# Tile statistics taken by the finishing stage, and the order of Wq and the context at the start of two wide attentions

## What is computed

```python
def _layernorm(x, axis=-1, eps=1e-05):
    m = jnp.mean(x, axis=axis, keepdims=True)
    v = jnp.var(x, axis=axis, keepdims=True)
    return (x - m) / jnp.sqrt(v + eps)

x = x + _L0_attn_ref(_layernorm(x), ...)            # windowed self attention
x = x + _L0_xattn_ref(_layernorm(x), ctx_768, ...)  # 16 heads of 64
x = x + _L0_ffn_ref(_layernorm(x), ...)             # mixture, 2 of 8 choices
...                                                 # layers 1, 2 and 3 likewise
```

```python
q = x @ Wq; k = context @ Wk; v = context @ Wv
sim = jnp.einsum('bhid,bhjd->bhij', q, k) * SCALE
attn = jax.nn.softmax(sim, axis=-1)
return jnp.einsum('bhij,bhjd->bhid', attn, v) ... @ Wo + bo
```

## Time and profile before

| | |
|---|---|
| time, median of 3 runs | 2756.67 us (2753.91 to 2758.6) |
| the profiled execution | 2766.99 us, its span 2765.3 us |
| mean granted TensorE clock in it | 0.884 of full speed |
| PE busy | 2137.1 us (77%) |
| DVE busy | 1714.5 us (62%) |
| ACT busy | 1201.0 us (43%) |
| POOL busy | 617.3 us (22%) |

### The profile page before, as it was taken

The page is one execution under the profiler, slowest core; times in us unless marked ns, Lnnn a source line. Parts: engine busy times, 40 slices in busy tenths (PEclk is TensorE's granted clock), DMA queues, the critical chain, the costliest instruction groups (busy, mean ns, idle before and its releaser), DMA issues. The chain is left out here.

```text
span 2765.3 us, 28267 instructions
## 1 busy us (share of the span) xinstructions
PE 2137.1 (77%) x10151; PEld 1327.1 (48%) x10181; DVE 1714.5 (62%) x2529; ACT 1201.0 (43%) x1900; POOL 617.3 (22%) x349
## 2 busy tenths in 40 slices
PE   5688889595699979889473888888758979373894
PEld 3456556584223335668331444444535654252474
DVE  5554345424677745522464999999634776856665
ACT  2334322110276653311145899999713236302340
POOL 3321112120332101012114666564100210000100
PEclk8899799697899999879796999999869999696896
DMA  6553120243654300224200000000111000000001
GB/s 128 77 85 39 59 92 1 102 154 122 105 78 66 34 21 0 73 74 171 68 34 27 1 1 1 1 1 1 61 58 35 0 1 0 0 8 13 8 1 37
DMA packets 107529, 126.74 MB, mean 46 GB/s; under 512 B 14823, under 2 KB 98676, under 8 KB 106357
## 3 DMA queue, kind: packets, MB, share of 16 engines
q1 hardware_dynamic: 94404, 109.63, 17.7%
q10 hardware_dynamic: 10098, 7.71, 0.9%
q0 software_dynamic: 2880, 7.48, 0.7%
...
## 5 line engine op out<-in xcount | busy, mean ns | idle before, releaser
L3148 DVE TENSOR_TENSOR_SCAN l2s_h<-l2s_aw 128x2048 f32<-128x2048 f32 x64 | 290.0, 4532 | 5.2 <-ACT l2s_rs L3193 5.2
L3107 PE MATMUL l2s_big<-g_xn,g_ident 128*128 128x512 f32 x512 | 259.0, 608 | 11.5 <-ACT g_xn L3186 6.4
L3162 POOL TENSOR_SCALAR l2s_aw<-l2s_aw 128x2048 f32<-128x2048 f32 x64 | 211.0, 3298 | 10.3 <-DVE l2s_aw L3140 5.1
L582 DVE TENSOR_REDUCE l1at_nm<-l1at_s 128x1 f32<-128x512 f32 x256 | 162.2, 683 | 66.7 <-PE l1at_s L432 65.7
L3099 PE MATMUL l2s_c_ps<-g_ident,l2s_h 128*128 128x128 f32 x1024 | 148.9, 279 | 55.7 <-ACT g_xn L3186 37.0
L3099 PEld LDWEIGHTS l2s_c_ps<-g_ident,l2s_h 128*128 128x128 f32 x1024 | 117.3, 141 | 146.4 <-issue 86.7
L680 ACT ACTIVATE g_xn<-l1at_s 128x512 f32<-128x512 f32 x256 | 143.4, 598 | 82.2 <-PE l1at_s L456 81.7
L3186 ACT ACTIVATE g_xn<-l2s_c_ps,l2s_ct 128x512 f32<-128x512 f32 x256 | 163.0, 690 | 17.1 <-PE l2s_c_ps L3099 16.9
L582 DVE TENSOR_REDUCE l0at_nm<-l0at_s 128x2 f32<-128x384 f32 x128 | 70.0, 557 | 101.0 <-PE l0at_s L432 99.9
L3179 ACT ACTIVATE l2s_aw<-l2s_dt,l2s_A 128x2048 f32<-128x2048 f32 x64 | 128.3, 2006 | 0.0
L3107 PEld LDWEIGHTS l2s_big<-g_xn,g_ident 128*128 128x128 f32 x512 | 82.0, 190 | 81.8 <-ACT g_xn L3186 58.6
...
## 6 DMA issues: line engine op xcount, KB each, us to landing
l1f_w<-in_L_ffn_w_dram SPq DMA_DIRECT2D x16, 1024.0 KB
l0f_w<-L_ffn_experts_inter_dram SPq DMA_DIRECT2D x7, 1024.0 KB
l0f_w<-n_L_ffn_experts_out_dram SPq DMA_DIRECT2D x7, 1024.0 KB
...
```

The costliest lines, as they stand in the source:

```text
L582: V.tensor_reduce(nm[:, s % 2, qts[0]:qts[-1] + 1, r], s1[:, u % 3, 0:len(qts) * KEYS].rearrange("p (q k) -> p q k", k=KEYS), AX, ALU.max, ...
L3107: nc.tensor.matmul(acc[:, tb, :], ident[:], hCT[:, tb, :], start=n == 0, stop=n == NST - 1).then_inc(acc_done, 1)
L3148: V.tensor_tensor_scan(out=h_all[:, i % 2].rearrange("p c t -> p (c t)"), data0=dA[:, i % 2].rearrange("p c t -> p (c t)"), data1=wd[:, i ...
L3162: nc.gpsimd.tensor_scalar(wd[:, i % 3], wd[:, i % 3], 10.0, -10.0, ALU.min, ALU.max).then_inc(clipped, 1)
```

## The change

A tile `g_st` that all stages share holds the statistics of x's tiles, and `c["known"]` says how many of them the stage that just ended has already taken. The next stage's start takes the rest only.

```diff
+def tile_stats(nc, c, first, last):
+
+    for i in range(first, last):
+        ins = nc.vector.bn_stats(c["st"][:, i, :], c["x"][:, i, :])
+    c["known"] = last
+    return ins
...
-        st = S.sb("stats", [P, TILES, 6])
+        st, known = c["st"], c.pop("known", 0)
...
-                    for i in range(TILES):
+                    for i in range(0 if r else known, TILES):
...
-                    ch.step(ins)
+                    if r or known < TILES:
+                        ch.step(ins)
```

(`normalise`; `wide_cross_attention`, `mixture` and `quantised_ffn` have the same.) Who takes them, in the order of the code (`divide` of the self attentions, then the loops of the wide and the narrow attention, the mixtures' end, `quantised_ffn`):

```diff
                             divide(s - 1)
+                            if b and g == 2:
+                                tile_stats(nc, c, (b - 1) * QT, b * QT)
...
                         blocks.quantise(dve, t)
+                    if t:
+                        dve.wait_ge(y_added, t)
+                        tile_stats(nc, c, t - 1, t)
...
                             add(t - 1)
+                        if t >= 2 and not guarded:
+                            dve.wait_ge(y_added, t - 1)
+                            tile_stats(nc, c, t - 2, t - 1)
...
+                    finished = added
                     dve.wait_ge(back_loaded[q], 16 * choices)
...
+                    if q:
+                        dve.wait_ge(back_added, finished)
+                        tile_stats(nc, c, 4 * q - 4, 4 * q)
...
                         add(t - 2)
+                    if t >= 4:
+                        dve.wait_ge(y_added, t - 3)
+                        tile_stats(nc, c, t - 4, t - 3)
```

In the wide attentions the order of the banks and of PE's and ACT's work changes:

```diff
-            uses = [("ctx", 0, "a")] + [("k", j, "a") for j in range(NC // 2)] + [("wq", j, "a") for j in range(NC // 2)]
+            uses = [("wq", j, "a") for j in range(NC // 2)]
+            uses.insert(NC // 2 if norm_ctx else 0, ("ctx", 0, "a"))
+            ahead = len(uses) if norm_ctx else 1
+            uses += [("k", j, "a") for j in range(NC // 2)]
...
-                    turn_ctx()
+                    if not norm_ctx:
+                        turn_ctx()
+                    pe.wait_ge(q_loaded, 16)
+                    for j in range(NC // 2):
+                        turn_wq(j)
+                    if norm_ctx:
+                        turn_ctx()
                     emptied_wait(pe, "ctx", 0)
                     pe.wait_ge(k_loaded, 32)
                     for j in range(NC // 2):
                         project(0, "k", j)
-                    pe.wait_ge(q_loaded, 16)
-                    for j in range(NC // 2):
-                        turn_wq(j)
...
+                    if norm_ctx:
+                        act.wait_ge(col_loaded, 16 * 6)
...
+                    empty(act, "a", 0, ahead, E.copy, scaled, affine)
                     for r in range(2 if norm_ctx else 1):
                         act.wait_ge(var_ready, r + 1)
                         E.activation(tmp[:], tmp[:], ACT.Sqrt).then_inc(std_ready, 1)
-                    if norm_ctx:
-                        act.wait_ge(col_loaded, 16 * 6)
-                    empty(act, "a", E.copy, lambda dst, src, scale: E.activation(dst, src, ACT.Copy, scale=scale),
-                          lambda dst, src, cols: E.activation(dst, src, ACT.Identity, scale=cols[:, 0:1], bias=cols[:, 1:2]))
+                    empty(act, "a", ahead, len(uses), E.copy, scaled, affine)
```

More of the change, by code:

```diff
@@ L845, in wide_cross_attention @@
             bob = R.sb("bob", [P, DM]) if bo is not None else None
-            st, mean, rstd, tmp = R.sb("st", [P, TILES, 6]), R.sb("mean", [P, TILES]), R.sb("rstd", [P, TILES]), R.sb("tmp", [P, TILES])
+            st, known = c["st"], c.pop("known", 0)
+            mean, rstd, tmp = R.sb("mean", [P, TILES]), R.sb("rstd", [P, TILES]), R.sb("tmp", [P, TILES])
             var = R.sb("var", [P, TILES])
@@ L962, in _, with empty @@
                             fold_o(b, jj)
-                def empty(eng, who, plain, scaled, affine):
-                    for u, (kind, j, by) in enumerate(uses):
+                def empty(eng, who, first, last, plain, scaled, affine):
+                    for u in range(first, last):
+                        kind, j, by = uses[u]
                         if by != who:
@@ L1006, in _, with scaled, affine @@
                         E.activation(ctmp[:], ctmp[:], ACT.Sqrt).then_inc(cstd_ready, 1)
+                    if norm_ctx:
+                        act.wait_ge(col_loaded, 16 * 6)
+                    def scaled(dst, src, scale):
+                        return E.activation(dst, src, ACT.Copy, scale=scale)
+                    def affine(dst, src, cols):
+                        return E.activation(dst, src, ACT.Identity, scale=cols[:, 0:1], bias=cols[:, 1:2])
+                    empty(act, "a", 0, ahead, E.copy, scaled, affine)
                     for r in range(2 if norm_ctx else 1):
@@ L1019, in _ @@
                         cch = Chain(dve, ctx_step)
-                        for i in range(TILES // 2):
+                        for i in range(known, TILES // 2):
                             V.bn_stats(st[:, i, :], x[:, i, :])
@@ L1033, in _ @@
                     ch = Chain(dve, step)
-                    for i in range(TILES // 2 if norm_ctx else 0, TILES):
+                    for i in range(max(known, TILES // 2 if norm_ctx else 0), TILES):
                         ins = V.bn_stats(st[:, i, :], x[:, i, :])
-                    ch.step(ins)
+                    if known < TILES:
+                        ch.step(ins)
                     row_stats_to_affine(nc, ch, st, mean[:], rstd[:], tmp[:], DM // 2)
@@ L1889, in _ @@
                     V = nc.vector
-                    for i in range(TILES):
+                    for i in range(known, TILES):
                         ins = V.bn_stats(st[:, i, :], x[:, i, :])
-                    ch.step(ins)
+                    if known < TILES:
+                        ch.step(ins)
                     row_stats_to_affine(nc, ch, st, mean[:], rstd[:], tmp[:], DM // 2)
@@ L3524, in decoder_kernel @@
         c["xnT"] = S.sb("xnT", [P, KC, TOK])
+        c["st"] = S.sb("st", [P, TILES, 6])
         x_stored = S.sem("x_stored")
```

5 lines of the change are left out of this document (2 added, 3 removed).

## The result

The changed kernel took 2733.69 us (median of 4 runs, 2730.52 to 2736.85) against 2757.64 for the kernel before (4 runs, 2753.91 to 2762.83): a ratio of 0.991, with a 95% interval of 0.9891 to 0.9928. That is 24 us less, where 2734.2 and 22.5 us less had been forecast. The comparison was repeated in another session: 2733.25 against 2760.79, ratio 0.9895 (0.988 to 0.9909), 27.5 us less. The ratios with their intervals are taken over the runs as a whole and lie up to 0.0008 from the quotient of the two medians.

What follows compares the result with a forecast made beforehand. No engine was busy throughout; stage starts, wide-attention preparation (clock) and tile loops bound it. Terms 11.4 + 0 + 4.5 + 0 + 0 + 4.6 - 3.9 + 2.9 + 3.0 = 22.5 us, off 2756.67: 2734.2 us, range 2725 to 2746.

Steps and rivals of the forecast that it cites:

- Part 1: l0x: Wq's transposes ahead of Wk's product fill PE's gap and raise the clock for that product; gain 11.4 us.
- Rival B: l0x: the product with Wk stays at 1.2 GHz, gain there only 1.9 us, total 2743.7; chance 0.18.
- Part 2: l2x: same reordering, Wk's product 1.8 us later and still cold, fold starting earlier but cold; net 0.
- Rival C: l2x: the clock is up for Wk's product and the fold too, 9.9 us more gain, 2724.3; chance 0.07.
- The page's rule: Wk's product, l0x and l2x: sustained activity alone releases the throttle; the order would be worth only 3.0 us.
- Part 3, the loops: l0x, l1x, l2x, l2f loops: 56 moved statistics fit DVE's idle time; cost 0 except at the last tile.
- rival E: Loops: added statistics exceed DVE's idle 0.80 us and delay every tile, 2765.8 us; chance 0.04.
- Part 3, the self attentions: Self attentions: 24 statistics in bursts of four are regained; cost 0, or 8 us if PE waits out each.
- rival D: Starts held by a DMA or table load, or self-attention bursts not covered; about 2742 us; chance 0.10.
- Part 4: Stage starts with fewer statistics: l0f 4.5, l1f 4.6, l2f 2.9, l3a 3.0 us gained; l2a -3.9; l1a, l1b 0.

Runs made afterwards that it cites:

- experiment 2: Changed kernel with only the new order of Wq, context and Sqrt, every stage taking all 16 statistics at its start: 2744.05 us against 2763.47, ratio 0.9938.
- experiment 4: Changed kernel with 36 unread transposes filling PE's idle time ahead of the product with Wk in l2x: 2726.31 us, ratio 0.9867.
- experiment 6: The changed kernel run again without edits, beside the others on one chip: 2733.25 us, 27.5 us less than the kernel before.
- experiment 7: Changed kernel with the four context scale and bias columns of l2x issued from SP ahead of Wk: 2736.96 us, ratio 0.9913.
- experiment 3: Changed kernel with only the moved statistics, Wq and Wk in the order of before: 2744.88 us, ratio 0.9937.
- experiment 10: Changed kernel with l2x's six column transfers issued by SP in l2s's first block: 2728.76 us, ratio 0.989.
- experiment 8: Changed kernel with three more unread statistics in every tick of the l0x and l2x loops: 2733.22 us (one run).
- before, again: The kernel before, with no edit, profiled a second time: 2755.46 us.
- experiment 12: The kernel before with an unused tile of 768 bytes a partition allocated, no instruction changed: 2760.21 us, ratio 0.9999.
- experiment 5: The kernel before with the shared statistics tile (384 bytes a partition) allocated but unused, no instruction changed: 2754.90 us, ratio 0.9974.

## Why the prediction was right, point by point

- **Part 1, l0x, 11.4 us.** Right in its mechanism and to 1.5 us in size: 12.9, and 11.6 to 12.8 in the five other profiles with this start in which the clock rose. K started 8.9 us after the stage's start (as before: 301.31 less 292.43; forecast 0.5 later), since the clock rose in Wq's transposes and shortened them; where they ran cold (experiments 2, 4, 6 and 7) K started at 9.2. POOL's addition beside DVE's copies, taken at 0.4, cost nothing that shows: DVE's 16 copies took 6.80 us, as before.
- **Rival B** wasn't excluded but happens in some executions: one of seven profiled. Its price is visible in experiment 6: 3.6 us of l0x's gain are left, 9.2 less than in the change (forecast 1.9 left, 9.5 less). The chance I gave it, 0.18, describes executions rather than kernels. Its ground, that the rise might come too late, was sound: in experiments 4 and 7 it came 5.5 and 5.3 us after the first of Wq's transposes, when K was running already.
- **Part 2, l2x, 0 us.** Right, term by term: K 1.5 us late (forecast 1.8), PE idle ahead of it for 4.4 us (5.3), 18.04 at 0.50, a fold slowed by 9.39 - 7.18 = 2.2 us (1.4 to 2.3). Rival C's condition was met on purpose in experiment 4, where K and fold together were 10.3 us shorter than in the change (9.9).
- **The page's rule,** by which K's own activity should have released the throttle (the Trainium skill, "TensorE: Matmul & The Clock Gate", Part 1: The HAM clock gate), was contradicted for K once more: in experiments 3 and 10 K stays at 0.50 for its 18 us, back to back, and in experiment 4, begun in l2x at 1.00, it stays there. For the fold the rule does hold: behind a cold K, in ten stages of these profiles, the clock rose 1.7 to 4.3 us after the fold's start each time. What tells K from the fold and the transposes, these runs don't show.
- **Part 3, the loops, 0.** Right, for more than the reason given: experiment 8 shows slack of at least another 1.0 us. The decision point of rival E, the idle 0.80 us, was placed too early.
- **Part 3, the self attentions, 0.** Right to half a microsecond. The first and the last addition of l1at, in "before, again" and then in the change:

```profile
830.14 1.28 DVE L611 TENSOR_TENSOR g_x<-g_x,l1at_m_ps 128x512 f32<-128x512 f32 x2
...
1010.60 0.69 DVE L611 TENSOR_TENSOR g_x<-g_x,l1at_m_ps 128x512 f32<-128x512 f32 x1 [1.04 <-PE l1at_m_ps L501]
```

```profile
809.74 1.27 DVE L620 TENSOR_TENSOR g_x<-g_x,l1at_m_ps 128x512 f32<-128x512 f32 x2
...
990.65 0.69 DVE L620 TENSOR_TENSOR g_x<-g_x,l1at_m_ps 128x512 f32<-128x512 f32 x1 [1.04 <-PE l1at_m_ps L510]
```

  All three bursts of l1at lie between these two rows. They are 180.46 us apart without bursts (so in four of the five profiles without them; 181.9 in experiment 12) and 180.91 with them (180.9 in all nine profiles that have them): the three bursts cost 0.4 us, and rival D's condition, a burst not covered, wasn't met. The rest of the +1.9 in the table had arisen ahead of the first burst. Up to the first addition PE waits 15.9 us for the keys' DMA in the change and 12.0 in "before, again"; what lengthens that wait stays open.
- **Part 4.** l0f 4.2 (4.5), l1f 4.3 (4.6), l2f 2.9 (2.9: 3.2 at its start, less 0.3 in l2x's last tick), l3a 3.9 (3.0: the larger end was right), l1f's end 3.6 (3.9). l0f's body with l1a's start is 1.1 us longer (0), as it is in experiment 5, which changes no instruction. l1x is 1.2 us longer in the change, but as much in experiments 2 and 12, which move no statistic there, so it isn't the edit; in all three the clock fell 118.4 to 118.5 us after its first product, in place of 122.2 to 122.4 in the kernel before, both times, and in experiment 5.
- **What wasn't forecast:** 6 us that come with the tile itself. Against the kernel with the unused tile (2754.90), the change's own instructions bring 21.6 us in the same session, where 22.5 had been summed. Of the 24 us of the first comparison some 6 are then the tile's, which no term had. That the total came within 2 us of the forecast is in part luck: executions with a late or missing rise in l0x, and what l0f, l1at and l1x had more in the change, took about what the tile gave.
- **Slips that cost nothing.** By the working given, a lone statistic is 5.32 less 15 times 0.33, or 0.37 us and not 0.41; the traces have 0.41 to 0.43. PE's transposes in l2x would end at 2050.3 by the terms given, not 2050.6. Rival E counts 53 statistics in the loops where part 3 has 56.
